# Last two groups of weighted values moved into the next batch's body, in a fused attention and FFN kernel

## The chip, the cores and the metric

The kernel runs on one core of a Trainium2 chip. The metric is the device time in microseconds of one execution, and lower is better. All numbers here are microseconds unless marked otherwise. TensorE is called PE, VectorE DVE, ScalarE ACT, GpSimd POOL, and the queue that issues the DMAs is SyncE (SP).

## The reference

There are 32 batches. In each, 112 query tokens attend to 375 context tokens: 257 image tokens and 118 text tokens, with a softmax of its own for each of the two sets.

```
q = rms_norm(layernorm(x) @ q_w.T + q_b) * norm_q_w        # 16 heads of 32
k, v         = from the 118 text tokens;  k_img, v_img = from the 257 image tokens
out = attention(q, k_img, v_img) + attention(q, k, v)
x   = x + out @ o_w.T + o_b
h   = layernorm(x);  score = h @ w_router                  # one number for each token
# the 14 tokens of each batch with the highest scores (32 * 14 = 448 rows) pass
# through one attention block (16 heads of 128, causal) and a gated MLP of width 2048,
# and their rows of x + h are replaced by the gated result
```

Everything is float32. The kernel splits each operand of the large products into a rounded part ("hi") and a rest ("lo") and multiplies three times (hi·hi, hi·lo, lo·hi).

## The kernel before, in words

There are three phases. The first makes the queries of all batches (to about 120 us). The second runs over the 32 batches. The third handles the 448 selected rows. The change is in the second phase and at its two ends.

Every engine has its own instruction list, written out by hand, and the engines meet only through semaphores. Nothing is reordered at run time, so an instruction whose semaphore isn't there yet also holds everything behind it on its engine. `over_batches` (L351) runs, on each engine, `pre()`, two bodies written out, a hardware loop for batches 2 to 29, one more body, and `last()`. A body has the arguments i (the batch), n = i + 1 (its keys and values are projected one body ahead), m = i + 2 (its context is loaded) and p = i - 1 (its output is finished one body late).

On PE a body (L1688) is made of these blocks:

- `scores(i, g)` for the four groups g of four heads: four matmuls, which are only used for the row maxima that DVE finds with two reductions (`group_max`, L1110 and L1111). `turn_top` transposes two groups of maxima, ACT copies them to `topT`.
- `keys(n, k)` for k = 0 to 2 and `values(n, k)` for k = 0 to 2: twelve matmuls of 512 columns each. Keys are evacuated by DVE (`add_bias`, L1090), squared and summed by ACT (`squares`, L783), the sum is raised to the power -0.5 by POOL (`inverse_rms`, L549), and DVE multiplies by it (`scale_k`, L1096). After that PE transposes them (`turn`, L1549), and ACT copies them into `k_hi` and `k_all` (`split_kq`), which the next body's first `scores` waits for.
- `scores_T(i, g)`: the scores again, transposed, with the maxima subtracted. There is one set of PSUM banks (2 to 5) for them. ACT takes the exponentials in two instructions (`exps`, L807 and L809) into `prob[:, g % 2]`, and `scores_T(i, g + 1)` may only start when both are done. POOL adds the two image parts (`sum_image`, L555), and DVE adds one more row (`add_tail`, L1116).
- `weighted_values(i, g, n)`: six sets of eight small matmuls (L1638), into bank 6 or 7. DVE divides (`normalise`: reciprocal L1122, product L1124, sum L1128).
- `output(p)`: the output projection of batch p. Its input is `oT`, rounded by ACT (`o_hi`) and by DVE (`o_rest`, L1132).

After `output(p)`, DVE adds the residual (`add_residual`, `ln2`), POOL makes the layernorm (`normalise_h`), DVE the score (`score`, L1159), POOL the sum that is stored (`output` on POOL, L559), PE transposes the scores (`turn_score`), and DVE ranks the tokens (`ranks`, L1150). POOL also adds the output bias to the loaded x (`residual`, L563), and makes the low part of the next batch's context (`split_ctx`, L522).

The PE order of one body before is: scores 0, values(i, 2), scores 1, output(p), scores 2, turn_top 0, keys 0, scores 3, keys 1, turn_top 1, scores_T 0, keys 2, turn_score(p), scores_T 1, weighted 0, first half of values(n, 0), scores_T 2, weighted 1, scores_T 3, second half of values(n, 0), weighted 2, weighted 3, turn 1 to 3, values(n, 1).

Of the kernel before, what the change touches and what calls it, by code (L numbers as in the profile page):

```python
# [48 lines left out]
RANK_BANK = (None, 6, 0)  # L49
HEADS = [*range(FH, FH + FKV), *range(FH)]  # L50
# [5 lines left out]
def build(nc, t, out):  # L56
    with ExitStack() as ctx:
# [124 lines left out]
        tok_junk = p1("tok_junk", [L, D], BF16)  # L182

# [73 lines left out]
        over_cos_k = ExitStack()  # L257
        attn_lo = over_cos_k.enter_context(nc.sbuf_tensor("attn_lo", [P, 2, S], F32R))
# [79 lines left out]
        def key_slot(n, k):  # L338
            if k == 2:
                return b1_full, b1_done, bank1, 3 * n - 1 if not isinstance(n, int) or n else 0  # L340
            return b0_full, b0_done, bank0, 4 * n + k // 2

        def value_slot(n, k):
            if k == 1:
                return b1_full, b1_done, bank1, 3 * n if not isinstance(n, int) or n else 1
            return b0_full, b0_done, bank0, 4 * n + 2 + k // 2

        def o_slot(i):
            return 3 * i + 4 if not isinstance(i, int) or i < B - 1 else 3 * B - 1

        def over_batches(eng, pre, body, last):  # L351

            pre()
            body(0, 1, 2, None)
            body(1, 2, 3, 0)
            with eng.Fori(2, B - 2) as i:
                body(i, i + 1, i + 2, i - 1)
            body(B - 2, B - 1, None, B - 3)
            last(B - 1, B - 2)
# [3 lines left out]
        PIECE_AT = {5 * j // 2: j + 2 for j in range(PIECES - 2)}  # L363

# [9 lines left out]
        def _(sp):  # L374
# [92 lines left out]
            def body(i, n, m, p):  # L467

                if m is not None:
                    sp.wait_ge(ctx_lo_done, 2 * m)  # L470
                    load_ctx(m)
                if p is not None:
                    store(p)
                    sp.wait_ge(xh_stored, 16 * i)
                sp.dma_start(xh[:, 0], t["x"][bass.ds(i, 1)].rearrange("o t d -> t (o d)")).then_inc(xres_loaded, 16)
                sp.wait_ge(st_full, 4 * i + 4)
                load_q(n)
                sp.wait_ge(pv_full, 4 * n)
                load_tail(n)

            def last(i, p):
                sp.wait_ge(b1_full, value_slot(i, 1)[3] + 1)
# [35 lines left out]
        def _(pool):  # L518
            def split_ctx(n):
                for part, cols in enumerate(CTX_PARTS):  # L520
                    pool.wait_ge(ctx_hi_done, 2 * n + part + 1)
                    nc.gpsimd.tensor_tensor(ctx_lo[:, :, cols], ctx_raw[:, :, cols], ctx_hi[:, :, cols].bitcast(F32), ALU.subtract).then_inc(ctx_lo_done, 1)  # L522
# [28 lines left out]
            def sum_image(i, g):  # L551
# [3 lines left out]
                nc.gpsimd.tensor_tensor(prob_img[:, g % 2], prob[:, g % 2, 1, :], prob[:, g % 2, 2, :], ALU.add).then_inc(img_summed, 1)  # L555
# [66 lines left out]
            def body(i, n, m, p):  # L622
                split_ctx(n)
                if p is not None:
                    normalise_h(p)
                inverse_rms(n, 1)
                if p is not None:
# [7 lines left out]
                if p is None:  # L635
                    pool.wait_ge(out_rows_loaded, 16 * 2)
                pool.wait_ge(tail_added, 4 * i + 4)
                residual(i)
# [16 lines left out]
            def last(i, p):  # L655
# [4 lines left out]
                for c in range(EARLY):  # L660
                    gather(c)
                pool.wait_ge(oT_lo_done, i)
                value_weights_lo(0, 0)
                value_weights_lo(0, 1).then_inc(w_lo_done, 1)
                normalise_h(p)
# [79 lines left out]
        def _(act):  # L745
# [53 lines left out]
            def turn_top(i, e):  # L799
                act.wait_ge(top_full, 2 * i + e + 1)  # L800
                nc.scalar.activation(topT[e][:], ps[:, 7, e * L:(e + 1) * L], ACT.Copy).then_inc(topT_ready, 1)

            def exps(i, g):
                act.wait_ge(st_full, 4 * i + g + 1)
                if g >= 2:
                    act.wait_ge(pv_full, 4 * i + g - 1)
                nc.scalar.activation(prob[0:CHUNK_C, g % 2, 0, :].rearrange("p (j q) -> p j q", j=GH),  # L807
                                     ps[0:CHUNK_C, 2:6, 0:L], ACT.Exp).then_inc(exp_done, 1)
                nc.scalar.activation(prob[:, g % 2, 1:3, :].rearrange("p c (j q) -> p j c q", j=GH),  # L809
# [10 lines left out]
            def value_text(i):  # L820
                act.wait_ge(b0_full, 4 * i + 4)
                nc.scalar.activation(v_txt[0:TXT], bank0[0:TXT], ACT.Copy).then_inc(b0_done, 1)
# [5 lines left out]
            def pre():  # L828
# [45 lines left out]
                value_image(0, 0)  # L874

            def body(i, n, m, p):
                value_image(i, 1)
                if p is not None:
                    o_hi(p)
                else:  # L880
                    act.wait_ge(consts_ready, 3)
# [13 lines left out]
                value_image(n, 0)  # L895
# [24 lines left out]
            def last(i, p):  # L920
                value_image(i, 1)
                o_hi(p)
                value_weights_hi(0)
                value_weights_hi(1)
                token_squares(0)
                turn_top(i, 0)
                turn_top(i, 1)
                token_squares(1)
                exps(i, 0)
                value_text(i)  # L930
# [134 lines left out]
        def _(dve):  # L1065
# [47 lines left out]
            def add_tail(i, g):  # L1113
                dve.wait_ge(img_summed, 4 * i + g + 1)
                last_rows = slice(P - HD, CHUNK_C)
                nc.vector.scalar_tensor_tensor(prob_img[last_rows, g % 2], prob[last_rows, g % 2, 0, :], ones_last[last_rows, 0:1],  # L1116
# [45 lines left out]
            def pre():  # L1162
# [47 lines left out]
                dve.wait_ge(rows_ready, 1)  # L1210
                add_bias(0, 1)
                add_bias(0, 2)
                scale_k(0, 1)
                add_bias(0, 3)
                scale_k(0, 2)
# [17 lines left out]
            def place(rows, turn):  # L1233
                dve.wait_ge(before_full, turn)
                dve.wait_ge(chosen_ready, turn)
                nc.vector.scalar_tensor_tensor(before[:, rows], chosen[:, rows], -FAR, ps[0:L, RANK_BANK[turn], rows], ALU.mult, ALU.add).then_inc(hot_ready, 1)
# [5 lines left out]
            def tokens(chunks, turn):  # L1242
                dve.wait_ge(tok_full, turn)
                nc.vector.tensor_tensor(tok[:, chunks], ps[0:L, RANK_BANK[turn], B + chunks.start:B + chunks.stop], token_base[:, chunks], ALU.add).then_inc(tok_ready, 1)

            def body(i, n, m, p):
                group_max(i, 0)
                if m is None:
                    dve.wait_ge(topk_loaded, 16 * 3)
                    choose(slice(0, EARLY_B), 1)  # L1250
                if p is not None:
                    o_rest(p)
                group_max(i, 1)
                if p is not None:
                    add_residual(p)
                group_max(i, 2)
                if p is None:
                    dve.wait_ge(pro_full, 2)
                    nc.vector.tensor_copy(v_tail, ps[0:B, 6, :]).then_inc(pro_done, 1)
                if p is not None:  # L1260
                    ln2(p)
                if m is None:
                    place(slice(0, EARLY_B), 1)
                group_max(i, 3)
# [747 lines left out]
```

## Time and profile before

| what | value |
|---|---|
| three runs, median (lowest, highest) | 1547.8 (1545.67, 1549.24) |
| span of the profiled execution | 1546.9 |
| PE busy | 1515.9 (98%) |
| DVE busy | 1186.4 (77%) |
| ACT busy | 712.3 (46%) |
| POOL busy | 665.3 (43%) |

The page gives the span as the profiled execution's time; the runs' median is 0.9 us above it. PE is busy nearly throughout, but its matmuls overlap in the record (the next one starts before the end of the one ahead), so a busy share does not tell how much work stands between two points. The distances between starts do, and the rows further down are mostly rows of the timeline for that reason.

### The profile page before, as it was taken

The page shows a single profiled execution, that of the slowest core. Times are in us where ns is not written, and L with a number is a line of the kernel's source. Part 1 is how long each engine was busy: PE and PEld are TensorE (multiplying, and loading weights), DVE is VectorE, ACT ScalarE, POOL GpSimd, SP SyncE. Part 2 cuts the span into 40 slices and gives each one's busy share as a digit, 9 for nine tenths or more (in the row PEclk, how much of TensorE's full clock was granted, in tenths as well). Part 3 has the DMA queues.
Part 4 walks back from the last instruction along what each step waited for, and adds up shares of the span by engine and source line. Part 5 has one row for each costly group of instructions (what it writes and reads, how often), then busy time and mean ns, then how long its engine had stood idle before and what let it go on. Part 6 is the DMA issues. An engine that isn't in the chain of part 4 may idle for free.

```text
span 1546.9 us, 41175 instructions
## 1 busy us (share of the span) xinstructions
PE 1515.9 (98%) x16220; PEld 1179.0 (76%) x16220; DVE 1186.4 (77%) x1884; ACT 712.3 (46%) x1458; POOL 665.3 (43%) x727
## 2 busy tenths in 40 slices
PE   8999999999999999999999999999998999999997
PEld 6777777777777777777777777777776787778897
DVE  6765888888887888888788888788887587554986
ACT  5874444444444344444444444434446124556431
POOL 3443434444434444433444443444445592114752
PEclk9999999999999999999999999999999999999999
DMA  8963111221111221111122111122114524010000
GB/s 265 337 201 124 52 52 53 78 61 50 56 50 50 69 69 54 55 50 50 57 74 61 50 56 50 50 69 72 51 37 128 193 109 164 28 55 29 1 1 24
DMA packets 70199, 121.04 MB, mean 78 GB/s; under 512 B 21840, under 2 KB 36528, under 8 KB 68608
## 3 DMA queue, kind: packets, MB, share of 16 engines
q1 hardware_dynamic: 69312, 117.54, 23.4%
q0 software_dynamic: 832, 2.75, 0.6%
q8 instruction: 36, 0.59, 0.2%
q14 instruction: 19, 0.16, 0.0%
HBM read 89.93 MB, written 30.34 MB: 78 GB/s over the span
## 4 chain that ended last, share of the span: by engine, by line
PE 88%; ACT 4%; DVE 3%; DMA 2%; issue 1%; SPq 1%; POOL 1%; ACTq 0%; POOLq 0%; DVEq 0%
PE ps L1488 21%; PE ps L1490 18%; PE ps L1489 18%; PE ps L1638 8%; PE ps L1603 6%; PE ps L1549 3%; PE ps L1578 3%; PE ps L1609 2%; PE ps L1837 2%; PE ps L1854 2%; ACT prob L809 2%; DMA q_dram<-q_turned 2%; PE ps L1846 1%; ACT prob L807 1%; PE ps L1613 1%
## 5 line engine op out<-in xcount | busy, mean ns | idle before, releaser
L555 POOL TENSOR_TENSOR prob_img<-prob 128x448 f32<-128x448 f32 x124 | 145.3, 1172 | 211.6 <-ACT prob L809 211.6
L522 POOL TENSOR_TENSOR ctx_lo<-ctx_raw,ctx_hi 128x472 fp32r<-128x472 f32 (+1 forms) x62 | 111.6, 1825 | 243.5 <-ACT ctx_hi L750 243.5
L1122 DVE RECIPROCAL rec<-ps 128x224 f32<-128x224 f32 x128 | 199.2, 1556 | 7.5 <-PE ps L1638 3.8
L807 ACT ACTIVATE prob<-ps 119x448 f32<-119x448 f32 x128 | 69.6, 544 | 196.3 <-PE ps L1603 196.3
L1111 DVE TENSOR_REDUCE top<-ps 112x4 f32<-112x1028 f32 x128 | 156.3, 1221 | 0.0
L1116 DVE SCALAR_TENSOR_TENSOR prob_img<-prob,ones_last,prob_img 23x448 f32<-23x448 f32 x124 | 84.8, 684 | 72.9 <-POOL prob_img L555 70.9
L783 ACT ACTIVATE sq_junk<-proj 128x513 bf16<-128x513 f32 (+1 forms) x96 | 61.2, 637 | 169.1 <-DVE proj L1090 169.1
L1110 DVE TENSOR_REDUCE top<-ps 112x4 f32<-112x472 f32 x128 | 83.1, 649 | 61.3 <-PE ps L1578 61.2
L1603 PE MATMUL ps<-q_all,k_all 32*128 32x112 f32 (+1 forms) x3072 | 125.2, 274 | 1.9 <-issue 1.9
L809 ACT ACTIVATE prob<-ps 128x896 f32<-128x896 f32 x128 | 117.0, 914 | 0.0
L1488 PE MATMUL ps<-w_v_img_hi,ctx_hi 128*128 128x512 f32 x256 | 110.9, 433 | 0.0
L1488 PE MATMUL ps<-w_k_img_hi,ctx_hi 128*128 128x512 f32 x256 | 107.4, 420 | 0.0
L1603 PEld LDWEIGHTS ps<-q_all,k_all 32*128 32x128 f32 (+1 forms) x3072 | 105.3, 184 | 2.0 <-issue 2.0
L1489 PE MATMUL ps<-w_v_img_lo,ctx_hi 128*128 128x512 f32 x256 | 101.1, 395 | 0.0
L1490 PE MATMUL ps<-w_k_img_hi,ctx_lo 128*128 128x512 f32 x256 | 101.0, 395 | 0.0
L1489 PE MATMUL ps<-w_k_img_lo,ctx_hi 128*128 128x512 f32 x256 | 100.5, 393 | 0.0
L1490 PE MATMUL ps<-w_v_img_hi,ctx_lo 128*128 128x512 f32 x256 | 100.4, 392 | 0.0
L1490 PE MATMUL ps<-hT_hi,ring_lo 128*128 128x448 f32 x224 | 82.2, 367 | 0.0
L549 POOL TENSOR_TENSOR rstd<-sq_sum,neg_half 128x1 f32<-128x1 f32 x96 | 52.9, 551 | 54.7 <-ACT sq_junk L783 54.7
L795 ACT ACTIVATE k_hi<-ps 128x512 fp32r<-128x512 f32 (+1 forms) x96 | 57.9, 603 | 23.0 <-PE ps L1549 22.9
L1395 DVE TENSOR_REDUCE neg_top<-ps 112x1 f32<-112x112 f32 (+1 forms) x64 | 28.4, 444 | 50.6 <-PE ps L1838 50.4
L707 POOL TENSOR_TENSOR ring_lo<-ring,wo_hi 128x512 fp32r<-128x512 f32 x16 | 20.6, 1286 | 97.0 <-ACT wo_hi L1000 97.0
(339 smaller groups left out, 4334.1 us busy)
## 6 DMA issues: line engine op xcount, KB each, us to landing
ctx_raw<-in_ctx_dram SPq DMA_DIRECT2D x32, 748.0 KB, 4.2
xh_dram<-xh SPq DMA_DIRECT2D x32, 448.0 KB, 3.1
xc<-in_xT_dram SPq DMA_DIRECT2D x28, 256.0 KB, 4.5
q_dram<-q_turned SPq DMA_DIRECT2D x28, 256.0 KB, 4.6
q_all<-q_dram SPq DMA_DIRECT2D x32, 224.0 KB, 3.1
out_dram<-out_sb SPq DMA_DIRECT2D x32, 224.0 KB, 2.3
xh<-in_x_dram SPq DMA_DIRECT2D x31, 224.0 KB, 2.9
proj<-in_x_dram SPq DMA_DIRECT2D x21, 256.0 KB, 5.2
```

Source lines behind the costliest of these rows:

```text
L522: nc.gpsimd.tensor_tensor(ctx_lo[:, :, cols], ctx_raw[:, :, cols], ctx_hi[:, :, cols].bitcast(F32), ALU.subtract).then_inc(ctx_lo_done, 1)
L555: nc.gpsimd.tensor_tensor(prob_img[:, g % 2], prob[:, g % 2, 1, :], prob[:, g % 2, 2, :], ALU.add).then_inc(img_summed, 1)
L807: nc.scalar.activation(prob[0:CHUNK_C, g % 2, 0, :].rearrange("p (j q) -> p j q", j=GH), ps[0:CHUNK_C, 2:6, 0:L], ACT.Exp).then_inc(exp_do ...
L809: nc.scalar.activation(prob[:, g % 2, 1:3, :].rearrange("p c (j q) -> p j c q", j=GH), ps[:, 2:6, L:3 * L].rearrange("p j (c q) -> p j c q ...
L1111: nc.vector.tensor_reduce(rows[:, :, 2 * g + 1], ps[0:L, 2:6, TAIL:CTX], AX.X, ALU.max).then_inc(s_done, 1)
L1116: nc.vector.scalar_tensor_tensor(prob_img[last_rows, g % 2], prob[last_rows, g % 2, 0, :], ones_last[last_rows, 0:1], prob_img[last_rows, ...
L1122: nc.vector.reciprocal(rec[:], bank[:, 2:4]).then_inc(norm_step, 1)
L1488: nc.tensor.matmul(o_, a_hi, b_hi, start=start, stop=False)
L1489: nc.tensor.matmul(o_, a_hi, b_lo, start=False, stop=False)
L1490: return nc.tensor.matmul(o_, a_lo, b_hi, start=False, stop=stop)
L1603: made = nc.tensor.matmul(ps[0:rows, 2 + j, c * L:(c + 1) * L], k_all[head, g, at:at + rows], q_all[head, g, :], start=False, stop=stop)
L1638: last = nc.tensor.matmul(ps[HD * j:HD * (j + 1), bank, slot * L:(slot + 1) * L], left[0:rows, cols], right[0:rows, L * j:L * (j + 1)], st ...
```

## The change

Batch p's groups 2 and 3 of `weighted_values` are done at the head of body i = p + 1, behind `scores(i, 0)`, and DVE's `normalise(p, 2)` and `normalise(p, 3)` move with them. For this the probabilities get a third buffer (`g % 3` in place of `g % 2`), made from `third_img` and `third_txt`. `output(p)` moves from the first part of the body to behind `scores_T(i, 3)`. Everything that follows it (`score`, `output` on POOL, `turn_score`, `ranks`, the stores) is done one body later, with a fifth argument q = i - 2. `values(n, 0)` is no longer halved and stands last, `values(i, 1)` moves into the body of its own batch, and banks 0 and 1 are dealt out anew. The transposed maxima go to bank 6 in place of bank 7.

The PE body, as the diff leaves it (for a body in the loop):

```
scores(i, 0)
weighted_values(p, 2, n); weighted_values(p, 3, n)
scores(i, 1); values(i, 2); scores(i, 2); values(i, 1)
turn_top(i, 0); scores(i, 3); keys(n, 0); turn_top(i, 1)
scores_T(i, 0); keys(n, 1)
wait pv_done 4 * i; turn_score(q)
scores_T(i, 1); keys(n, 2)
scores_T(i, 2)
weighted_values(i, 0, n)
wait rank_done q + 1
weighted_values(i, 1, n)
scores_T(i, 3)
output(p)
wait exp_done 8 * i + 8; turn(n, 1); turn(n, 2); turn(n, 3)
values(n, 0)
```

The core of the diff on the other engines:

```diff
 # SP
-    def body(i, n, m, p):
+    def body(i, n, m, p, q):
+                    sp.wait_ge(pv_full, 4 * i)
+                    load_tail(i)
+                    store(q)
+                    sp.wait_ge(xh_stored, 16 * q + 16)
+                    load_xres(p)
                     sp.wait_ge(ctx_lo_done, 2 * m)
                     load_ctx(m)
...
 # POOL
-                split_ctx(n)
-                    normalise_h(p)
+                split_ctx(n, 0)
+                    output(q)
+                split_ctx(n, 1)
+                sum_image(i, 0)
                 inverse_rms(n, 1)
-                    output(p)
-                sum_image(i, 0)
+                    residual(p)
+                sum_image(i, 1)
                 inverse_rms(n, 2)
-                sum_image(i, 1)
                 inverse_rms(n, 3)
                 sum_image(i, 2)
                 sum_image(i, 3)
-                residual(i)
+                    normalise_h(p)
...
 # ACT
-                value_image(i, 1)
-                    o_hi(p)
-                value_text(i)
-                split_ctx(n, 0)
-                split_ctx(n, 1)
-                turn_top(i, 0)
-                squares(n, 1)
-                turn_top(i, 1)
-                exps(i, 0)
-                squares(n, 2)
-                exps(i, 1)
-                squares(n, 3)
-                exps(i, 2)
+                value_image(i, 0)
+                value_text(i)
+                split_ctx(n, 0)
+                split_ctx(n, 1)
+                value_image(i, 1)
+                turn_top(i, 0)
+                turn_top(i, 1)
+                exps(i, 0)
+                    o_hi(p)
+                squares(n, 1)
+                exps(i, 1)
+                squares(n, 2)
+                squares(n, 3)
+                exps(i, 2)
                 exps(i, 3)
                 split_kq(n)
-                value_image(n, 0)
...
 # DVE, a body in the loop, as the diff leaves it
+                group_max(i, 0)
+                group_max(i, 1);  normalise(p, 2)
+                group_max(i, 2);  score(q)
+                group_max(i, 3);  normalise(p, 3)
+                add_bias(n, 1);   o_rest(p)
+                add_tail(i, 0);   ranks(q)
+                scale_k(n, 1);    add_bias(n, 2)
+                scale_k(n, 2);    add_tail(i, 1)
+                add_bias(n, 3)
+                normalise(i, 0);  scale_k(n, 3)
+                normalise(i, 1);  add_tail(i, 2)
+                tail_keys(n);     add_residual(p);  ln2(p)
+                add_tail(i, 3)
```

In `pre()`, `values(0, 0)` moves ahead of `keys(0, 2)` and `values(0, 1)` leaves it for body 0, so that the transposes of batch 0 are followed at once by the scores. In `last()`, `values(i, 1)`, `score(q)`, `ranks(q)`, `output(q)` and `residual(p)` come in. The body of batch 30 also does its own groups 2 and 3.

## Rows read from the trace of the kernel before

**Rows 1.** Busy time by engine over the loop: stretch; busy (count); clock, DMA share, GB/s.

```profile
180.00:1210.00 1030.00, 1019.49 (x13398) 777.96 (x13387) 831.21 (x1265) 460.52 (x892) 441.53 (x463) 1.00 0.19 59
```

**Rows 2.** Timeline of PE, one body from values(n, 1) to the next: start, duration, instruction.

```profile
793.60 0.49 PE L1488 MATMUL ps<-w_v_img_hi,ctx_hi 128*128 128x512 f32 x1
...
796.58 0.43 PE L1578 MATMUL ps<-k_hi,q_hi 32*112 32x376 f32 x4
...
806.98 0.50 PE L1488 MATMUL ps<-w_k_img_hi,ctx_hi 128*128 128x512 f32 x1
...
809.86 0.26 PE L1585 MATMUL ps<-ident,top 112*128 112x112 f32 x1
810.05 0.32 PE L1609 MATMUL ps<-topT,pick_c 32*119 32x112 f32 x4
...
814.18 0.32 PE L1609 MATMUL ps<-topT,pick_c 32*119 32x112 f32 x4
...
815.24 0.40 PE L1638 MATMUL ps<-prob,v_last 119*32 119x112 f32 x8
...
816.53 0.50 PE L1488 MATMUL ps<-w_v_img_hi,ctx_hi 128*128 128x512 f32 x1
...
818.12 0.32 PE L1609 MATMUL ps<-topT,pick_c 32*119 32x112 f32 x4
...
820.73 0.32 PE L1609 MATMUL ps<-topT,pick_c 32*119 32x112 f32 x4 [0.19 <-ACT prob L809]
...
823.36 0.40 PE L1638 MATMUL ps<-prob,v_last 119*32 119x112 f32 x8
...
824.54 0.38 PE L1638 MATMUL ps<-prob,v_last 119*32 119x112 f32 x8
...
825.82 1.50 PE L1549 MATMUL ps<-ident,proj 118*128 118x118 f32 x12
827.07 0.49 PE L1488 MATMUL ps<-w_v_img_hi,ctx_hi 128*128 128x512 f32 x1
```

**Rows 3.** Timeline of ACT, same body: the squares of the keys, and an exponential.

```profile
809.59 0.64 ACT L783 ACTIVATE sq_junk<-proj 118x513 bf16<-118x513 f32 x1 [5.38 <-DVE proj L1090]
...
815.39 0.54 ACT L807 ACTIVATE prob<-ps 119x448 f32<-119x448 f32 x1 [2.17 <-PE ps L1603]
```

**Rows 4.** Timeline of POOL, same body: power, stored sum, image sum.

```profile
810.40 0.56 POOL L549 TENSOR_TENSOR rstd<-sq_sum,neg_half 128x1 f32<-128x1 f32 x1 [1.40 <-ACT sq_junk L783]
810.93 1.29 POOL L559 TENSOR_TENSOR out_sb<-xh 112x512 f32<-112x512 f32 x1
...
816.82 1.16 POOL L555 TENSOR_TENSOR prob_img<-prob 128x448 f32<-128x448 f32 x1 [2.38 <-ACT prob L809]
```

**Rows 5.** Timeline of DVE, same body: maxima, bias, scaling, ranks, normalise, tail row.

```profile
807.10 0.65 DVE L1110 TENSOR_REDUCE top<-ps 112x4 f32<-112x472 f32 x1 [0.43 <-PE ps L1578]
...
808.80 0.68 DVE L1090 TENSOR_TENSOR proj<-ps,k_bias 118x512 f32<-118x512 f32 x1
...
811.00 1.77 DVE L1096 SCALAR_TENSOR_TENSOR proj<-proj,rstd,w_txt 118x512 f32<-118x512 f32 x1 [0.24 <-POOL rstd L549]
...
815.29 0.74 DVE L1096 SCALAR_TENSOR_TENSOR proj<-proj,rstd,w_img 128x512 f32<-128x512 f32 x1
815.95 0.33 DVE L1150 SCALAR_TENSOR_TENSOR equal<-ps,score_now,later 112x112 f32<-112x112 f32 x1
...
816.67 1.56 DVE L1122 RECIPROCAL rec<-ps 128x224 f32<-128x224 f32 x1
...
819.06 0.68 DVE L1116 SCALAR_TENSOR_TENSOR prob_img<-prob,ones_last,prob_img 23x448 f32<-23x448 f32 x1
```

**Rows 6.** Timeline of the end of pre: transposes, scaling of the tail keys, first scores.

```profile
119.45 1.45 PE L1549 MATMUL ps<-ident,proj 118*128 118x118 f32 x12
...
121.99 0.74 DVE L1220 SCALAR_TENSOR_TENSOR o_space<-o_space,sq_sum,w_img 32x512 f32<-32x512 f32 x1 [1.67 <-POOL sq_sum L613]
...
126.97 0.43 PE L1578 MATMUL ps<-k_hi,q_hi 32*112 32x376 f32 x4
```

More of the change, by code:

```diff
@@ L661, in last @@
                     gather(c)
+                output(q)
                 pool.wait_ge(oT_lo_done, i)
@@ L1210, in pre @@
                 dve.wait_ge(rows_ready, 1)
+                add_bias(0, 2)
                 add_bias(0, 1)
[L1212 removed]
                 scale_k(0, 1)
+                scale_k(0, 2)
                 add_bias(0, 3)
[L1215 removed]
                 scale_k(0, 3)
@@ L1250, in body @@
                     choose(slice(0, EARLY_B), 1)
+                group_max(i, 1)
+                if p is not None:
+                    normalise(p, 2)
+                else:
+                    dve.wait_ge(pro_full, 2)
+                    nc.vector.tensor_copy(v_tail, ps[0:B, 6, :]).then_inc(pro_done, 1)
+                group_max(i, 2)
+                if q is not None:
+                    score(q)
+                group_max(i, 3)
+                if p is not None:
+                    normalise(p, 3)
+                add_bias(n, 1)
                 if p is not None:
                     o_rest(p)
[L1253 to L1261, printed above, removed]
+                add_tail(i, 0)
+                if q is not None:
+                    ranks(q)
+                scale_k(n, 1)
+                add_bias(n, 2)
                 if m is None:
                     place(slice(0, EARLY_B), 1)
-                group_max(i, 3)
-                add_bias(n, 1)
-                if p is not None:
-                    score(p)
-                add_bias(n, 2)
+                scale_k(n, 2)
+                add_tail(i, 1)
+                add_bias(n, 3)
                 if m is None:
                     tokens(slice(0, EARLY), 1)
-                scale_k(n, 1)
-                add_tail(i, 0)
-                add_bias(n, 3)
-                scale_k(n, 2)
-                if p is not None:
-                    ranks(p)
                 normalise(i, 0)
-                add_tail(i, 1)
                 scale_k(n, 3)
@@ L1281, in body @@
                 add_tail(i, 2)
+                tail_keys(n)
+                if p is not None:
+                    add_residual(p)
+                    ln2(p)
                 add_tail(i, 3)
-                normalise(i, 2)
-                tail_keys(n)
-                normalise(i, 3)
+                if m is None:
+                    normalise(i, 2)
+                    normalise(i, 3)
             def o_rest_part(i, g):
@@ L1300, in last @@
                 group_max(i, 1)
+                score(q)
                 group_max(i, 2)
+                group_max(i, 3)
                 add_residual(p)
-                group_max(i, 3)
                 ln2(p)
+                ranks(q)
+                normalise(i, 0)
                 score(p)
-                normalise(i, 0)
                 normalise(i, 1)
@@ L1584, in turn_top @@
                     pe.wait_ge(topT_ready, 2 * i + 1)
-                nc.tensor.transpose(ps[:, 7, e * L:(e + 1) * L], top[e][:], ident[0:L, 0:L]).then_inc(top_full, 1)
+                if not isinstance(i, int) or i:
+                    pe.wait_ge(pv_done, 4 * i - 1)
+                else:
+                    pe.wait_ge(pro_done, 2)
+                nc.tensor.transpose(ps[:, 6, e * L:(e + 1) * L], top[e][:], ident[0:L, 0:L]).then_inc(top_full, 1)
             def turn_score(p):
@@ L1654, in pre @@
                 pe.wait_ge(qp_done, NT - 1)
-                keys(0, 0)
+                keys(0, 1)
                 turn_q(NT - 2)
                 pe.wait_ge(qp_done, NT)
-                keys(0, 1)
+                keys(0, 0)
                 turn_q(NT - 1)
+                values(0, 0)
                 keys(0, 2)
@@ L1679, in count_before @@
                 pe.wait_ge(chosen_ready, turn)
-                nc.tensor.matmul(ps[0:L, RANK_BANK[turn], rows], later[:], chosen[:, rows], start=True, stop=True).then_inc(before_full, 1)
+                nc.tensor.matmul(rank_cols(turn, rows), later[:], chosen[:, rows], start=True, stop=True).then_inc(before_full, 1)
             def find_tokens(chunks, turn):
@@ L1716, in body @@
                 weighted_values(i, 0, n)
-                values(n, 0, range(0, 2))
-                scores_T(i, 2)
-                if p is not None:
-                    pe.wait_ge(rank_done, i)
+                if q is not None:
+                    pe.wait_ge(rank_done, q + 1)
                 weighted_values(i, 1, n)
                 scores_T(i, 3)
-                values(n, 0, range(2, 4))
-                weighted_values(i, 2, n)
-                weighted_values(i, 3, n)
+                if p is not None:
+                    output(p)
+                pe.wait_ge(exp_done, 8 * i + 8)
                 for k in range(1, 4):
                     turn(n, k)
-                values(n, 1)
+                if m is None:
+                    weighted_values(i, 2, n)
+                    weighted_values(i, 3, n)
+                values(n, 0)
             def output_part(i, g):
```

195 lines of the change are left out of this document (112 added, 83 removed).

## The prediction

> **What bounds the kernel now.** I read the busy time over the loop first: in 180 to 1210 PE is busy for 1019.49 of 1030, at a granted clock of 1.00, and DVE, the next engine, for 831.21, or 81% [rows 1]. PE's order is fixed, so the question is how long one body takes on PE, and whether a wait stands in it. For that I read PE's timeline from one start of values(n, 1) to the next. The reader should see three things there. A body takes 827.07 - 793.60 = 33.47. It has a single wait, in front of scores_T 3 at 820.73, where ACT's exponentials of group 2 come late [rows 2]. And the length of a block depends on its neighbour: twelve projection matmuls take 796.58 - 793.60 = 2.98 when scores follow, and 809.86 - 806.98 = 2.88 when a transpose follows. The last three views are the timelines of ACT, POOL and DVE, for the time that each link between two blocks takes.
>
> **What PE wins.** All blocks of the body stay, in another order, so PE's gain is in the seams and in the one wait.
>
> - values(n, 0) is whole again. Its halves take 818.12 - 816.53 = 1.59 and, behind a scores_T of 815.24 - 814.18 = 1.06, 823.36 - (820.73 + 1.06) = 1.57. Together that is 3.16 against 2.98: 0.18 won.
> - weighted 0 and 1 become neighbours. Such a block takes 824.54 - 823.36 = 1.18 ahead of another of its kind, and 816.53 - 815.24 = 1.29 (or 825.82 - 824.54 = 1.28) ahead of anything else: 0.11 won.
> - values 1, output and keys 0 will be followed by a transpose (up to 0.10 won each), keys 2 no longer (0.10 lost), and turn_top 0 is followed by scores (I take 0.06 lost). Net 0.11.
> - The wait goes: scores_T 2 to scores_T 3 is 820.73 - 818.12 = 2.61, of which 1.06 + 1.29 is work. 0.26 won, if nothing else is late there.
>
> That is 0.40 in seams and 0.26 of wait; a body without any wait would take 33.47 - 0.66 = 32.81.
>
> **What is late next.** Count from the start of scores_T 1 in the changed body. PE has behind it keys 2 (2.98), scores_T 2 (1.06), weighted 0 (1.18) and weighted 1 (1.29, with 1.06 for scores_T 1 itself): scores_T 3 could start at 7.57. It needs the exponentials of group 2. In ACT's order these stand behind squares(n, 3), as before, but keys 2, whose squares they are, stood ahead of scores_T 1 and now stands behind it, and so do the squares and powers of keys 1. squares(n, 3) needs add_bias(n, 3), which DVE has behind scale_k(n, 2) and add_tail(i, 1), and POOL makes the factor of scale_k(n, 2) only behind sum_image(i, 1). So there is a chain through all four engines, and each link has a row:
>
> - scores_T 1 to its exponential: 815.39 - 814.18 = 1.21 [rows 2, 3]
> - exponential to sum_image: 816.82 - 815.39 = 1.43; its length 1.16 [rows 3, 4]
> - inverse_rms and scale_k: 811.00 - 810.40 = 0.60 [rows 4, 5]
> - scale_k to the next on DVE: 815.95 - 815.29 = 0.66; add_tail 0.68 and about 0.02; add_bias 0.68 [rows 5]
> - end of add_bias to squares: 809.59 - (808.80 + 0.68) = 0.11; squares 0.64 [rows 3, 5]
> - exponential of group 2 to scores_T 3: 2.61 - 1.21 = 1.40, since before this pair was what PE waited for [rows 2].
>
> The sum is 8.59 against 7.57: PE waits 1.02 in each body. Before, the add_bias of the third keys did not stand behind a scale_k that waits for sum_image 1.
>
> **Two collisions make the chain longer.** The trace shows scale_k in two sizes: 0.74 with POOL idle, and 1.77 at 811.00, while POOL's stored sum runs from 810.93 to 812.22. It ends 0.55 after POOL does [rows 4, 5]. So DVE instructions with both inputs in SBUF stand still while POOL works on whole tiles. The changed order has this twice ahead of add_bias(n, 2). scores_T 0 starts 814.18 - 810.05 = 4.13 before scores_T 1. Its exponentials start at -2.92 and its sum_image at -1.49, which lasts to -0.33. o_rest waits for o_hi, which ACT starts only behind those exponentials, about -1.7, and thus meets the sum_image; it ends at -0.33 + 0.55 = 0.22. add_tail 0 follows to 0.92. Then POOL's residual(p), as long as the stored sum (1.29), runs beside ranks (816.67 - 815.95 = 0.72) to 2.2, and scale_k(n, 1), due at 1.64, ends at 2.2 + 0.55 = 2.75. add_bias(n, 2) ends at 3.43, its squares start at 3.54, POOL's power 810.40 - 809.59 = 0.81 later at 4.35, and scale_k(n, 2) at 4.95. Without the collisions it would start at 1.21 + 1.43 + 1.16 + 0.60 = 4.40. That is 0.55 more: PE waits for 1.02 + 0.55 = 1.57. I take 1.5, since sum_image, o_rest and add_tail don't all start at the worst moment. The bounds are 1.02 (no collision) and 1.9 (each blocked instruction pays its full 0.74 behind POOL's end, not 0.55, in both places).
>
> The Trainium skill bears on this ("SBUF — State Buffer", section "Who interferes with whom"): a DVE instruction with two SBUF inputs and a GpSimd instruction that reads SBUF share a port pair that one of them holds for its whole length, while the other is blocked, and the order of issue decides which. The 1.77 above agrees; by the rule taken to the letter the blocked one would still pay its full length, so that the wait would be 1.57 + 2 x 0.19 = 1.95.
>
> **What is covered.** Ahead of scores_T 1 I find no wait, but little room. group_max takes 808.80 - 807.10 = 1.70 of DVE and normalise 819.06 - 816.67 = 2.39 [rows 5]. scores 1 comes behind scores 0 and two weighted blocks, at about 2.8, and group_max 0 ends about 2.4. scores 3 needs group_max 2, which stands behind normalise(p, 2): about 9.2 against 9.5. keys 1 needs POOL's low part of the image context, which stands behind output(q): about 13.7 against 14.0. Each of these, if missed, costs its excess in every body, a few tenths. The DMAs (the tail row, both stores, the load of x behind the stores, the context) are issued in SP's new order long ahead of their uses; the load of x, the one that is moved past others, waits for output(q) at about 11.2 and is used at about 17. q's load follows scores_T 3 as before, and the block that covers it grows from one half of the values and two weighted blocks to the output, which is about as long. DVE's own list ends some 1.5 ahead of the next group_max.
>
> **The ends.** Before, the transposes of batch 0 start at 119.45 and the scores at 126.97: 7.52, filled with two value blocks of 2.98 [rows 6]. Now both blocks are elsewhere. What remains is the chain of the tail keys: their scaling ends 121.99 + 0.74 - 119.45 = 3.28 behind the transposes, and four transposes, a copy and the tail columns follow (about 1.0), so the scores start at about 4.3, of which 7.52 - 5.96 = 1.56 is work. That is 2.7 of new wait, once. In last() work comes in on DVE and POOL, and I find no term there that I can price; I take 0, with 3 on either side.
>
> **The sum.** A body in the loop changes by 1.5 - 0.40 - 0.26 = +0.84. 29 of 31 bodies have the collisions, the first two lack them (+0.36): 24.4 + 0.7 = 25.1. With 2.7 at the start it is +27.8, on a span of 1546.9: 1574.7. The median of the runs stands 0.9 above the span, so I predict 1575. Between a wait of 1.3 and 1.9 this is 1568 to 1590, and that is the likeliest case's own range.
>
> **Rivals.**
>
> - No collisions: the order of arrival spares o_rest and scale_k, and only the chain of 1.02 is left. 31 x 0.36 + 2.7 = +13.9: 1561.7, and 1556 to 1567 with the seams off by 0.2. For it speaks that POOL and DVE are met only once in the body before; against it that sum_image 0 and o_rest are released by neighbouring ACT instructions. 22%.
> - Faster: the chain fits in PE's shadow. The place is squares(n, 3) ahead of exps(i, 2), the price is 0.66 won per body. It decides from a chain under 7.57 + 0.66 = 8.23 on; if the chain is under 7.57, the whole is 31 x -0.66 + 2.7 = -17.8, or 1530; between them 1530 to 1547. It needs my sum of 8.59 to be wrong by 0.4 to 1.0. For it speaks only that the sum has ten links and that POOL's spans are rough. 18%.
> - One of the early waits (scores 3, keys 1) is missed as well, by about 0.3 in each body: 1575 + 9 = 1584, to 1595. Against it are the two margins of 0.3. 10%.
>
> The forecast itself has 47%. No change (within 0.2%, 3 us, which is about what three runs can tell) lies in the gap between the rivals: 3%. So slower has 47 + 22 + 10 = 79%, faster 18%. The range leaves out the faster rival: 1555 to 1592.
>
> **What would show it.** In the changed kernel's PE timeline: a wait of 1.0 to 1.9 in front of scores_T 3, released by ACT's L809, in each body, and a body of 34.3; on ACT, squares(n, 3) directly ahead of exps 2, released by DVE; on DVE, o_rest and the first scale_k lengthened, and two scale_k of 0.74. A body of 32.8 would show the chain covered, one of 33.9 the chain without the collisions. The first scores should start about 4.3 behind the first transposes of batch 0.

## The result, and the profile after

The changed kernel takes 1582.68 (1580.93 to 1583.98, four runs) against 1547.32 before in the same series: 1.0231 times the time before, with an interval of 1.0219 to 1.0243. It is slower by 35.4, where the forecast was +27.8. A body of the loop costs 0.75 more, where the forecast was 0.84. The two ends cost more than I gave them.

The busy times of the page after, and of the loop (stretch; busy and count of PE, PE's weight loads, DVE, ACT, POOL; clock; DMA share; GB/s):

```profile
span 1582.3 us, 41380 instructions
...
PE 1506.9 (95%) x16220; PEld 1190.6 (75%) x16220; DVE 1210.7 (77%) x1884; ACT 712.2 (45%) x1458; POOL 704.1 (44%) x727
```

```profile
180.00:1210.00 1030.00, 988.92 (x13059) 772.41 (x13058) 842.70 (x1235) 451.38 (x875) 468.62 (x454) 1.00 0.19 57
```

Against [rows 1], PE is busy 30 less in the same stretch at the same clock, so it waits. The waits of PE in a third of the loop (line, releaser: total, times, longest), and then one body of its timeline, from scores 0 to scores 0:

```profile
PE ps L1650 <- ACT third_img L840: 12.4, 9, 1.4
```

```profile
783.70 0.43 PE L1615 MATMUL ps<-k_hi,q_hi 32*112 32x376 f32 x4
784.06 0.40 PE L1681 MATMUL ps<-third_txt,v_last 119*32 119x112 f32 x8
...
800.85 0.32 PE L1650 MATMUL ps<-topT,pick_c 32*119 32x112 f32 x4
...
804.88 0.32 PE L1650 MATMUL ps<-topT,pick_c 32*119 32x112 f32 x4
...
805.94 0.40 PE L1681 MATMUL ps<-prob,v_last 119*32 119x112 f32 x8
...
807.12 0.38 PE L1681 MATMUL ps<-prob,v_last 119*32 119x112 f32 x8
...
809.84 0.32 PE L1650 MATMUL ps<-topT,pick_c 32*119 32x112 f32 x4 [1.38 <-ACT third_img L840]
...
813.77 1.44 PE L1586 MATMUL ps<-ident,proj 118*128 118x118 f32 x12
...
817.93 0.43 PE L1615 MATMUL ps<-k_hi,q_hi 32*112 32x376 f32 x4
```

There is one wait in the body, in front of scores_T 3 at 809.84, in place of the 0.19 of [rows 2]. The body takes 817.93 - 783.70 = 34.23. It was 33.48 before, by the distance of the scores. The chain that holds ACT, on DVE, ACT and POOL in the same body:

```profile
799.76 1.31 DVE L1163 TENSOR_TENSOR oT_lo<-o_space,oT_hi 128x448 fp32r<-128x448 f32 x1 [1.35 <-ACT oT_hi L858]
...
802.55 0.93 DVE L1127 SCALAR_TENSOR_TENSOR proj<-proj,rstd,w_txt 118x512 f32<-118x512 f32 x1
803.41 0.68 DVE L1121 TENSOR_TENSOR proj<-ps,ki_bias 128x512 f32<-128x512 f32 x1
805.51 0.76 DVE L1127 SCALAR_TENSOR_TENSOR proj<-proj,rstd,w_img 128x512 f32<-128x512 f32 x1 [1.42 <-POOL rstd L573]
806.30 0.68 DVE L1147 SCALAR_TENSOR_TENSOR prob_img<-prob,ones_last,prob_img 23x448 f32<-23x448 f32 x1
807.02 0.69 DVE L1121 TENSOR_TENSOR proj<-ps,ki_bias 128x512 f32<-128x512 f32 x1
```

```profile
802.05 0.54 ACT L838 ACTIVATE prob<-ps 119x448 f32<-119x448 f32 x1 [1.71 <-PE ps L1644]
...
804.12 0.64 ACT L811 ACTIVATE sq_junk<-proj 128x513 bf16<-128x513 f32 x1 [0.72 <-DVE proj L1121]
...
807.82 0.64 ACT L811 ACTIVATE sq_junk<-proj 128x513 bf16<-128x513 f32 x1 [2.97 <-DVE proj L1121]
...
808.45 0.53 ACT L838 ACTIVATE third_txt<-ps 119x448 f32<-119x448 f32 x1
```

```profile
799.43 1.16 POOL L580 TENSOR_TENSOR prob_img<-prob 128x448 f32<-128x448 f32 x1 [2.34 <-ACT prob L840]
800.54 0.94 POOL L573 TENSOR_TENSOR rstd<-sq_sum,neg_half 128x1 f32<-128x1 f32 x1
801.45 1.48 POOL L588 TENSOR_TENSOR xh<-xh,out_bias 112x512 f32<-112x512 f32 x1
803.48 1.16 POOL L580 TENSOR_TENSOR prob_img<-prob 128x448 f32<-128x448 f32 x1 [0.55 <-ACT prob L840]
804.93 0.55 POOL L573 TENSOR_TENSOR rstd<-sq_sum,neg_half 128x1 f32<-128x1 f32 x1 [0.28 <-ACT sq_junk L811]
```

The reader sees ACT idle for 2.97 until DVE's third add_bias (807.02 + 0.69), and the exponential of group 2 start at 808.45, although its scores had been ready since about 806.1. DVE in turn stood 1.42 until 805.51 for POOL's power.

**Where the 35.4 went.** By the starts of the scores in both profiles, the 28 bodies of the loop take 958.5 in place of 937.7: +20.8. The other 14.6 lie at the ends. The first scores start at 131.76 in place of 126.97, although values(0, 1), 2.98 of work, had left that stretch. That is 7.8 later than the work asks for. Of these, 2.3 come from the query phase ahead of it: its last transposes start at 115.72 in place of 113.43, with the same code. (They start between 112.1 and 114.2 in the profiles of the ten experiments further down, so the 2.3 are no effect of the change.) The other 5.5 are two new waits, 1.89 in front of the transposes of the tail's keys and 3.46 in front of the first scores. Body 0 takes 35.93 in place of 33.33, though it has lost two weighted blocks (2.47). It has a wait of 1.02 in front of scores_T 3, one of 1.48 in front of its transposes, and one of 0.89 behind it, in front of body 1's scores. Body 1 adds 0.6, body 30 is 4.7 longer, of which 2.47 moved in, and the rest is 1.9 longer with 2.98 moved in.

The end of pre and the beginning of body 0 on PE (in `pre()`, keys(0, 0) and keys(0, 1) also change places, which are the same amount of work):

```profile
124.53 1.44 PE L1586 MATMUL ps<-ident,proj 118*128 118x118 f32 x12
...
127.86 0.43 PE L1713 MATMUL ps<-ident,o_space 32*128 32x32 f32 x4 [1.89 <-DVE o_space L1251]
...
131.76 0.66 PE L1615 MATMUL ps<-k_hi,q_hi 32*112 32x376 f32 x4 [3.46 <-ACT k_all L824]
...
132.78 0.63 PE L1526 MATMUL ps<-w_v_img_lo,k_tail_hi 128*32 128x512 f32 x1
133.21 0.63 PE L1527 MATMUL ps<-w_v_img_hi,k_tail_lo 128*32 128x512 f32 x1
```

From the first transposes to the first scores it is still 7.23, against 7.52 in [rows 6], but now PE waits for most of it. The releaser of the longer wait is ACT's last copy of the keys. ACT, POOL and DVE in the changed kernel, and ACT in the kernel before:

```profile
127.52 0.52 POOL L645 MEMSET v_last<- 119x512 f32 x1
...
128.07 0.58 ACT L817 ACTIVATE q_hi<-q_all 128x448 fp32r<-128x448 f32 x1 [1.91 <-POOL v_last L645]
...
128.83 0.16 DVE L1134 COPY k_all<-k_tail 128x4 f32<-128x4 f32 x1
...
130.87 0.63 ACT L824 ACTIVATE k_all<-ps 128x512 f32<-128x512 f32 x1
```

```profile
122.99 0.58 ACT L789 ACTIVATE q_hi<-q_all 128x448 fp32r<-128x448 f32 x1 [1.91 <-POOL v_last L620]
...
125.79 0.64 ACT L796 ACTIVATE k_all<-ps 128x512 f32<-128x512 f32 x1
```

The last column of the tail's keys (DVE at 128.83) is ready 2.5 before the copies end. The copies end 6.97 behind the first transposes in the changed kernel and 6.98 before. So the chain was as long before, and 7.5 of work on PE covered it. Behind the waits the matmuls of 512 columns start 0.43 apart, not 0.23: PE runs at the lower of its two clocks (1.2 GHz), and the granted clock is 0.88 of full speed over 132 to 150. The Trainium skill gives 426.7 ns for the distance of such matmuls at 1.2 GHz ("TensorE: Matmul & The Clock Gate", section "Wait — 56ns, not 53.3ns?"); the rows agree.

### The profile page after: what moved, and what is told of

Read it like the earlier page. It is cut to its first block, busy times and chain, and to the rows that moved or that the text cites. A ratio compares the mean times of both kernels' runs of the same rounds, so it can differ in the third digit from the quotient of the medians.

```text
span 1582.3 us, 41380 instructions
## 1 busy us (share of the span) xinstructions
PE 1506.9 (95%) x16220; PEld 1190.6 (75%) x16220; DVE 1210.7 (77%) x1884; ACT 712.2 (45%) x1458; POOL 704.1 (44%) x727
## 4 chain that ended last, share of the span: by engine, by line
PE 67%; DVE 9%; POOL 8%; ACT 7%; issue 7%; DMA 2%; POOLq 0%; ACTq 0%; DVEq 0%
PE ps L1525 16%; PE ps L1526 14%; PE ps L1527 14%; PE ps L1681 5%; POOL prob_img L580 4%; PE ps L1644 3%; PE ps L1615 3%; POOL xh L588 3%; PE ps L1586 2%; PE ps L1887 2%; ACT prob L840 2%; DVE proj L1127 2%; PE ps L1904 2%; ACT third_img L840 2%; DVE prob_img L1147 2%
## 5 line engine op out<-in xcount | busy, mean ns | idle before, releaser
L580 POOL TENSOR_TENSOR prob_img<-prob 128x448 f32<-128x448 f32 x93 | 107.6, 1157 | 123.0 <-ACT prob L840 123.0
L573 POOL TENSOR_TENSOR rstd<-sq_sum,neg_half 128x1 f32<-128x1 f32 x96 | 64.6, 673 | 115.9 <-ACT sq_junk L811 112.8
L838 ACT ACTIVATE prob<-ps 119x448 f32<-119x448 f32 x96 | 52.4, 546 | 124.4 <-PE ps L1644 124.4
L1525 PE MATMUL ps<-w_v_img_hi,ctx_hi 128*128 128x512 f32 x256 | 106.8, 417 | 0.0
L840 ACT ACTIVATE prob<-ps 128x896 f32<-128x896 f32 x96 | 87.7, 914 | 0.0
L1127 DVE SCALAR_TENSOR_TENSOR proj<-proj,rstd,w_img 128x512 f32<-128x512 f32 x64 | 49.9, 780 | 46.2 <-POOL rstd L573 46.2
L778 ACT ACTIVATE ctx_hi<-ctx_raw 128x472 fp32r<-128x472 f32 x64 | 52.9, 827 | 69.8 <-PE ps L1527 69.8
L1650 PEld LDWEIGHTS ps<-topT,pick_c 32*119 32x119 f32 x512 | 23.5, 173 | 77.4 <-ACT third_img L840 48.1
L1650 PE MATMUL ps<-topT,pick_c 32*119 32x112 f32 x512 | 40.6, 307 | 41.0 <-ACT third_img L840 40.8
```

Source lines behind the costliest of these rows:

```text
L580: nc.gpsimd.tensor_tensor(prob_img[:, g % 2], image[:, 0, :], image[:, 1, :], ALU.add).then_inc(img_summed, 1)
L840: nc.scalar.activation(image.rearrange("p c (j q) -> p j c q", j=GH), ps[:, 2:6, L:3 * L].rearrange("p j (c q) -> p j c q", c=2), ACT.Exp) ...
L1127: nc.vector.scalar_tensor_tensor(proj[0:rows, k - 1, 0:D], proj[0:rows, k - 1, 0:D], rstd1[0:rows, k:k + 1], (w_txt if k == 1 else w_img)[ ...
L1525: nc.tensor.matmul(o_, a_hi, b_hi, start=start, stop=False)
```

## The experiments

All are made from the changed kernel.

**The third add_bias early.**

```diff
 # DVE
+                add_bias(n, 3)
                 scale_k(n, 2)
                 add_tail(i, 1)
-                add_bias(n, 3)
```

> Changed kernel with DVE's add_bias(n, 3) moved ahead of scale_k(n, 2) and add_tail(i, 1). Theory (the chain through scale_k 2, add_tail 1, add_bias 3, squares 3 holds the exponentials of group 2): add_bias 3 can start 0.1 behind the end of keys 2 (about 4.1 behind scores_T 1 in place of 6.2), squares 3 ends before scores_T 2's results are there, the wait of 1.38 in front of scores_T 3 goes, a body takes 34.23 - 1.43 = 32.8, and with 31 bodies the median is 1582.7 - 44 = 1538. Rival (the wait is set by something else, such as POOL's sum_image or the exponentials themselves, or another wait takes its place at once): body 34.0 to 34.2, median 1575 to 1583.

Measured: 1535.28 (1534.61 to 1537.6), 0.9926 of the time before (0.9907 to 0.9945). PE's timeline:

```profile
752.78 0.43 PE L1615 MATMUL ps<-k_hi,q_hi 32*112 32x376 f32 x4
...
773.96 0.32 PE L1650 MATMUL ps<-topT,pick_c 32*119 32x112 f32 x4
...
777.47 0.32 PE L1650 MATMUL ps<-topT,pick_c 32*119 32x112 f32 x4
...
785.56 0.43 PE L1615 MATMUL ps<-k_hi,q_hi 32*112 32x376 f32 x4
```

A body takes 32.78, without any wait of PE in the loop. One line turned a loss of 2.3% into a gain of 0.7%. The time fell by 47.4, more than the 44 expected. Between the two profiles bodies 0 to 30 give 45.0 (40.7 in the loop); what else differs between them lies in stretches with the same code. The chain through scale_k 2, add_tail 1 and add_bias 3 is what cost the loop its time, and nothing took its place.

**The exponentials ahead of the squares.**

```diff
 # ACT
-                squares(n, 3)
                 exps(i, 2)
+                squares(n, 3)
```

> Changed kernel with ACT's exps(i, 2) ahead of squares(n, 3), DVE and POOL as they are. Theory (PE waits only because the exponentials stand behind squares 3 in ACT's list): the same wait of 1.38 goes although add_bias 3 stays late, body 32.8, median 1538; squares 3 then starts as late as it does now (3 behind scores_T 2) and scale_k 3 is still in time for the transposes. Rival (lateness of the DVE chain costs anyway, then in front of the transposes): a wait of 0.5 to 1.4 moves in front of turn, body 33.3 to 34.2, median 1553 to 1583.

Measured: 1535.85 (1535.42 to 1537.43), 0.9928 (0.991 to 0.9946), body 32.78. The starts of scores_T 1, the last exponential of group 2, add_bias 3, squares 3 and scores_T 3:

```profile
770.34 0.32 PE L1650 MATMUL ps<-topT,pick_c 32*119 32x112 f32 x4
...
776.02 0.91 ACT L840 ACTIVATE third_img<-ps 128x896 f32<-128x896 f32 x1
...
776.52 0.69 DVE L1121 TENSOR_TENSOR proj<-ps,ki_bias 128x512 f32<-128x512 f32 x1
...
777.32 0.64 ACT L811 ACTIVATE sq_junk<-proj 128x513 bf16<-128x513 f32 x1 [0.38 <-DVE proj L1121]
...
777.89 0.32 PE L1650 MATMUL ps<-topT,pick_c 32*119 32x112 f32 x4
```

Here add_bias 3 is as late as in the changed kernel (it starts 6.18 behind scores_T 1, squares 3 at 6.98), and PE doesn't wait. So the lateness itself costs PE nothing. It costs only through ACT's order, which puts the urgent exponentials behind the late squares; e1 takes away the lateness, e2 the order, and either is enough. The rival, a wait in front of the transposes, falls.

**Both collisions away, and each by itself.** e3 has both edits, e5 only the one on DVE, e6 only the one on POOL.

```diff
 # POOL
-                    residual(p)
                 sum_image(i, 1)
...
                 sum_image(i, 2)
+                    residual(p)
                 sum_image(i, 3)
 # DVE
-                    o_rest(p)
                 add_tail(i, 0)
...
                 add_bias(n, 3)
+                    o_rest(p)
                 normalise(i, 0)
```

> Changed kernel without the two collisions of DVE and POOL ahead of add_bias(n, 2): POOL's residual(p) moved between sum_image 2 and 3, DVE's o_rest(p) moved behind add_bias(n, 3). Theory (the chain alone costs about 1.0 of waiting and the collisions the rest): the wait in front of scores_T 3 falls from 1.38 to 1.0 or 1.1, body 33.9, median 1582.7 - 31 x 0.35 = 1572. Rival A (the collisions are the cause of the whole wait): wait near 0, median 1540. Rival B (they cost nothing on this path, since sum_image 1 and the power behind it end last): wait 1.38, median 1582.

> Changed kernel with only DVE's o_rest(p) moved behind add_bias(n, 3); residual(p) stays. Theory (of the 0.34 that both moves gave, nearly all is o_rest, which ran 1.31 in place of 0.62 beside sum_image 0 and had DVE wait for ACT): body 33.9 to 34.0, wait in front of scores_T 3 1.0 to 1.1. Rival (scale_k 1 beside residual(p) is the one that counts): body 34.1 to 34.2.

> Changed kernel with only POOL's residual(p) moved between sum_image 2 and 3; o_rest stays. Theory: scale_k 1 ran 0.93 beside the end of residual(p) and 0.75 without, so at most 0.18 is won: body 34.05 to 34.15. Rival (residual(p) is the collision that counts): body 33.9.

| kernel | time | body | wait in front of scores_T 3 |
|---|---|---|---|
| changed | 1582.68 | 34.23 | 1.38 |
| o_rest late (e5, single run) | 1568.5 | 33.90 | 1.05 |
| residual late (e6, single run) | 1575.76 | 34.03 | 1.18 |
| both (e3, 1.0150, 1.0129 to 1.0171) | 1570.6 | 33.89 | 1.04 |

Scores_T 3 in e5, e6 and e3, in this order:

```profile
766.46 0.32 PE L1650 MATMUL ps<-topT,pick_c 32*119 32x112 f32 x4 [1.05 <-ACT third_img L840]
```

```profile
769.28 0.32 PE L1650 MATMUL ps<-topT,pick_c 32*119 32x112 f32 x4 [1.18 <-ACT third_img L840]
```

```profile
766.32 0.32 PE L1650 MATMUL ps<-topT,pick_c 32*119 32x112 f32 x4 [1.04 <-ACT third_img L840]
```

With both gone 1.04 is left, the bare chain. The profile counts a wait from the modelled end of the last matmul; by starts, scores_T 3 stands 8.66 behind scores_T 1 in e3, where the work takes 7.57, and a body is 33.89 - 32.78 = 1.11 longer than in e1. So the chain costs 1.1, and I had priced it at 1.02. The collisions together are 0.34, and they don't add up (0.33 and 0.20), since from a certain point on sum_image 1 and the power behind it end last. The rival that they are the whole cause falls, and so does the one that they are nothing. The times of e5 and e6 are single runs, so these two rest on their profiles, where the wait is the same in all 28 bodies. For e6 I had expected less (34.05 to 34.15); residual(p) counts for a little more than its overlap with scale_k.

**The end of pre.** e4 fills the wait with values(0, 0); e7 takes away one of its causes, four fills on POOL that ACT's copies wait for.

```diff
 # e4, PE
                 turn_q(NT - 1)
-                values(0, 0)
                 keys(0, 2)
...
                     turn(0, k)
+                values(0, 0)
                 pe.wait_ge(tail_scaled, 1)
```

```diff
 # e7, POOL: the fills of k_hi, k_all, v_txt and v_last, with the waits ahead of them
                 inverse_rms(0, 2)
+                fills
                 inverse_rms(0, 3)
                 tail: add, power
-                fills
```

> Changed kernel with values(0, 0) put back between the transposes of batch 0 and the tail's transposes at the end of pre. Theory (the loss at the start is the missing cover for the copies and the tail keys, plus the half clock that follows the idle stretch): 3.0 of the 5.4 waited there are filled, and the stretch at half clock behind it (about 2) shrinks or goes, median 1582.7 - 3 to 5 = 1578 to 1580. Rival (the wait follows the last transposes whatever fills it, as when the query load or the zeroed tiles are late in absolute time): no change, 1582 to 1583.

> Changed kernel with POOL's four fills of k_hi, k_all, v_txt and v_last moved ahead of the third power of batch 0. Theory (at the start ACT's copies wait for these fills behind the tail's power, and everything to the first scores hangs on them): copies start 2.0 earlier, first transposes to first scores 5.2 in place of 7.2, and a shorter stretch at half clock: median 1582.7 - 2 to 4 = 1579 to 1581. Rival (the query load or the third transposes are as late): no change, 1582 to 1583.

Measured: e4 1577.7 (1575.96 to 1577.98), 1.0191 (1.0172 to 1.0210); e7 1579.39 (1577.15 to 1580.23), 1.0209 (1.0191 to 1.0227). By the medians 5.0 and 3.3 are won, as the theory had it, but the profiles show less. From the last query transposes to the first scores it is 16.04 in the changed kernel, 13.98 in e4 and 13.96 in e7, and body 0 takes 36.05 and 35.58 in place of 35.93. That is 1.9 and 2.4 won. The rest of the medians' difference lies in stretches with the same code, so the theory's direction is shown and its size is not. The intervals of e7 and of the changed kernel (1.0219 to 1.0243) overlap a little, so e7 rests on its profile:

```profile
121.83 1.45 PE L1587 MATMUL ps<-ident,proj 118*128 118x118 f32 x12
...
126.99 0.43 PE L1616 MATMUL ps<-k_hi,q_hi 32*112 32x376 f32 x4 [1.39 <-ACT k_all L825]
```

First transposes to first scores are 126.99 - 121.83 = 5.16, in place of 7.23. In e4 that length stays (7.37), but PE has 2.98 of work in it, and the transposes start 6.61 behind the last query transposes and not 8.8.

**Idle transposes in the waits.** e9 is the changed kernel, e10 is e1 with the same edit.

```diff
 # PE
+                for _ in range(12):
+                    nc.tensor.transpose(ps[:, 2, 0:P], ident[:], ident[:])
                 pe.wait_ge(tail_scaled, 1)
                 # the tail's four transposes
+                for _ in range(22):
+                    nc.tensor.transpose(ps[:, 2, 0:P], ident[:], ident[:])
```

> Changed kernel with 12 idle transposes on PE ahead of the tail's transposes at the end of pre and 22 behind them, where PE otherwise waits 1.9 and 3.5; nothing else is moved, and no waiting instruction is taken away. Theory (the wait itself stays, but the stretch at half clock behind it goes: about 20 matmuls at 0.43 apart in place of 0.23 to 0.24): same 7.2 from the first transposes to the first scores, granted clock 1.00 behind it, median 1582.7 - 2 = 1580 to 1581. Rival (the half clock costs nothing that counts, since body 0 has waits of its own): 1582 to 1583.

> As e1_bias_up (add_bias(n, 3) early) with the same 34 idle transposes. Theory: 1535.3 - 2 = 1533 to 1534, body 32.78, granted clock 1.00 in 120 to 150. Rival: 1535.3, no gain.

Measured: e9 1578.49 (1578.27 to 1579.41), 1.0214 (1.0197 to 1.0231); e10 1533.92 (1532.78 to 1535.87), 0.9928 (0.9912 to 0.9945). The clock over the two stretches (the last fields but two), first in the changed kernel, then in e9:

```profile
120.00:132.00 12.00, 6.64 (x41) 4.44 (x39) 3.32 (x7) 5.37 (x12) 2.27 (x7) 0.90 0.75 268
132.00:150.00 18.00, 18.00 (x105) 11.36 (x105) 8.42 (x10) 4.63 (x9) 3.79 (x3) 0.88 0.11 33
```

```profile
120.00:132.00 12.00, 10.50 (x74) 7.55 (x73) 4.87 (x9) 5.37 (x12) 2.27 (x7) 1.00 0.74 266
132.00:150.00 18.00, 18.00 (x138) 12.99 (x137) 8.67 (x11) 6.72 (x13) 5.52 (x5) 1.00 0.14 48
```

The first scores stand as far behind the transposes as before (7.24), and body 0 takes 34.31 in place of 35.93, which is 1.6 less. Work without any use kept the half clock away from the start of body 0. Up to scores_T 3 of body 0 that gave 2.0. Of this 0.4 was lost again behind the waits of 1.02 and 1.48, where e9 runs at half clock and the changed kernel, with the same two waits, does not (1.00 over 158 to 161). In e9:

```profile
158.00:161.00 3.00, 2.67 (x13) 2.67 (x14) 2.84 (x7) 1.25 (x4) 1.13 (x1) 0.50 0.34 76
```

The same happens in e4 (0.61 over 158 to 162), which is why its body 0 is no shorter. Bodies 0 and 1 of e10 take 65.7 in place of e1's 67.4, so the gain is 1.7 there. In the timed runs the gain can't be told from none: the intervals of e9 and the changed kernel overlap, and e10 stands to its time before as e1 does. The profiles show it, and the times only agree with it.

**All together.** e8 has the edits of e1, e4 and e7.

> Changed kernel with three repairs together: add_bias(n, 3) ahead of scale_k(n, 2), values(0, 0) behind the transposes of batch 0, the four fills early. Theory (loop and start are separate losses and add up): body 32.78, first transposes to first scores about 5.2 with 3.0 of it filled, no stretch at half clock behind it: 1535.3 - 5.0 - 2 = 1528, that is 1526 to 1530. Rival (the repairs at the start overlap, since either alone already reaches the tail keys' chain): 1530 to 1533.

Measured: 1528.64 (1528.28 to 1529.48), 0.9887 of the time before (0.9870 to 0.9905). The loop is at 32.78, the first transposes to the first scores at 124.42 - 118.97 = 5.45, and the clock at 1.00 behind them. The two repairs at the start add up: from the last query transposes to the first scores it is 12.06, 3.98 less than 16.04, where e4 and e7 won 2.06 and 2.08 of this stretch. The rival falls. e8 beats both kernels, by 17.7 against the time before in its own series and by 54 against the changed kernel in the first one.

## Why the prediction was right

The direction, the place of the wait and the cost of a body were right. The size of the two ends was not.

**The seams.** I gave 0.40 for fewer and cheaper changes between kinds of blocks, and 0.26 for the wait: 32.81 for a body without waits. e1 and e2 measure it: 32.78. How the 0.40 splits among the seams was not tested.

**The chain.** Its ten links from [rows 2 to 5] came to 8.59 and a wait of 1.02; e3 measures 8.66 and a wait of 1.09 in the same terms (starts to starts). That the two are so close has some luck in it. I had taken 0.66 from scale_k to add_tail, from a row in which ranks follows; in e3 add_tail starts 0.78 behind scale_k. From the start of sum_image 1 to the power it was 1.11, not 1.16. The place, the releaser and ACT's squares directly ahead were as written.

**The collisions.** This term was mis-sized: 0.55 in the working, 0.48 taken, 0.34 measured. The mechanism was as written: scale_k 1 ended 0.55 behind the end of residual(p) (803.48 and 802.93). But POOL began residual(p) before add_tail 0 was done, so that it ended 2.08 behind scores_T 1 and not 2.2, although it took 1.48 in place of 1.29. From the end of scale_k 1 to squares 2 it was another 0.15 less than my links. So scale_k 2 started 4.66 behind scores_T 1, and I had 4.95. o_rest did as foretold: it ran beside sum_image 0 (799.43 to 800.59), took 1.31 (0.62 at 798.86 in the kernel before), and ended 0.48 behind it. The Trainium skill says that the second of the two is blocked until the first is done ("SBUF — State Buffer", section "Who interferes with whom"); the row agrees in the direction, but the blocked one doesn't pay its full 0.62 afterwards.

**What is covered.** The margins that I had called narrow held. In the loop, scores 3, keys 1 and the copies of the keys brought no wait, neither in the changed kernel nor in the faster bodies of e1. group_max 2 ended 0.5 ahead of scores 3, and POOL's low part 0.7 ahead of keys 1. Only behind body 0 the copies were late, by 0.9.

**The ends.** Here the prediction fell short: +2.7 in its sum, against 14.6 in the profile, of which 2.3 lie in unchanged code. The term that was mis-sized most is the start of the first scores, which I put 4.3 behind the transposes by way of the tail's keys. That path was sized well: the tail's last column was ready 4.5 behind the transposes. But ACT's copies of the keys, which wait for POOL's fills behind the tail's power, end later, and were not in the sum: the first scores came at 7.2. In [rows 6] the whole 7.52 stood there, and I took it for work because PE was busy through it; under that work lay a chain as long. The rest are terms that I had put at nothing: the half clock that follows such a wait (1.6); the new wait of 1.5 in front of body 0's transposes, which has no output to stand ahead of them; the 0.9 behind it; and the end of the loop. In body 30, PE waits 0.90 in front of weighted 0 (DVE's table of tokens, L1275), which it did not before, and in this execution it goes on at half clock behind it. The changed kernel, then e4, from the same place on:

```profile
1184.34 0.60 PE L1681 MATMUL ps<-prob,v_last 119*32 119x112 f32 x8 [0.90 <-DVE tok L1275]
```

```profile
1180.45 0.40 PE L1681 MATMUL ps<-prob,v_last 119*32 119x112 f32 x8 [0.90 <-DVE tok L1275]
```

The granted clock is 0.57 over 1184 to 1188 in the first and 1.00 over 1180 to 1184 in the second. That is why body 30 takes 38.83 here and 37.5 in e4, e5, e7 and e9.

That the total lies close to the forecast is in part luck. The 28 bodies of the loop cost 2.7 less than I had summed (20.8, not 23.5), and the ends about 12 more.

**The rivals.** "No collisions" fell: the collisions cost 0.34 in each body. Its loop is that of e3, where I had put them out of the way. "Faster" fell too, since it needed my sum to be wrong by 0.4 or more, and it was wrong by 0.07. But the same gain was there to be had with one line in another place. "An early wait as well" fell: the loop has one wait only.

What is still open: last() was not tried apart. From the first scores of batch 31 to the end it takes 1.1 less than before once the 2.98 that moved in are taken off, but that stretch varies from 381.7 to 385.8 among the ten experiments, which all have the same code there. Why the same waits are followed by half clock in one execution and not in another is open too.

## What to carry to other kernels

When work is moved so that one engine has fewer seams, list for each instruction it waits for what stands ahead of that one on its own engine, through every engine up to the first that is on time. The sum of such a chain from the old trace was good to 0.07 in 8.66. Moving one instruction, an add ahead of two that waited, or the exponentials ahead of the squares, was worth 1.45 in each body, some 45 in all. And a stretch in which the bound engine is busy throughout may hide a chain just as long: before its work is moved away, follow the chain.

## What the runs showed of the hardware

- The powers of one column on POOL, 0.55 by themselves, took 0.94 at 800.54, beside a DVE instruction with two SBUF inputs.
- A scale_k on DVE (two SBUF inputs, 0.74 alone) that met POOL's residual or stored sum ended 0.55 or 0.56 behind POOL's end in four places: 812.77 and 812.22 in the kernel before, 803.48 and 802.93 in the changed kernel, 759.95 and 759.40 in e5, 769.40 and 768.84 in e3.
- Behind waits of 1.9 and 3.5, with four small transposes between, PE went on at 1.2 GHz for some 4.5. The waits of 1.38 in the 28 bodies of the loop had no such effect (clock 1.00), and with 34 idle transposes in the two waits at the start it stayed at 2.4 GHz over 120 to 150.
- Other waits had it in some executions only: those of 1.02 and 1.48 in body 0 in e4 and e9 (clock 0.61 and 0.50 behind them) and not in the changed kernel (1.00), that of 0.90 in body 30 in the changed kernel (0.57) and not in e4 (1.00).
